# Products of probs and values issued in four runs per group of heads instead of ten single steps

## What is computed

```python
qkv = xn @ w_qkv.T + b_qkv                       # q, k, v: (2, 1024, 32, 16)
scores = einsum('bqhd,bkhd->bhqk', q, k) / 4 + alibi
scores = where(causal, scores, -1e9)
out = einsum('bhqk,bkhd->bqhd', softmax(scores), v)
s = out @ w_out.T + b_out
g = silu(octonion_ffn(xn, w_gate, w_up, w_down))
return x + s * g
```

## Time and profile before

| what | value |
|---|---|
| median of 3 runs | 965.25 us |
| the profiled execution, its own time | 966.12 us |
| its span, first to last instruction | 964.3 us |
| mean granted TensorE clock | 0.98 |
| TensorE busy | 905.3 us, 94% |
| VectorE busy | 648.4 us, 67% |
| ScalarE busy | 462.2 us, 48% |

### The profile page before, as it was taken

One profiled execution on the slowest core, in us unless ns is written; L12 is line 12 of the kernel. 1 busy time (PEld: TensorE's weight loads), 2 busy tenths in 40 slices (PEclk: granted clock), 3 DMA queues, 4 the chain that ended last, 5 costly groups with the idle time before them and its releaser, 6 DMA issues.

```text
span 964.3 us, 16724 instructions
## 1 busy us (share of the span) xinstructions
PE 905.3 (94%) x5630; PEld 483.2 (50%) x5630; DVE 648.4 (67%) x1425; ACT 462.2 (48%) x634; POOL 110.8 (11%) x119
## 2 busy tenths in 40 slices
PE   3696999999999996999999999999999999999987
PEld 3582457645854682444444444444444444443565
DVE  5678543543454442774888888888888888883488
ACT  3474532243223311124666666666666666667610
POOL 1121212130313032120000000000000000000042
PEclk9798999999999998999999999999999999999999
DMA  7322004201410138911256664546664456742757
GB/s 199 148 83 77 1 25 154 85 1 38 164 60 0 58 139 119 126 17 44 41 75 102 100 84 73 78 72 100 95 86 74 77 74 100 99 134 102 246 180 306
DMA packets 78177, 92.41 MB, mean 96 GB/s; under 512 B 26829, under 2 KB 43213, under 8 KB 78129
## 3 DMA queue, kind: packets, MB, share of 16 engines
q1 hardware_dynamic: 78017, 91.54, 43.7%
q0 software_dynamic: 112, 0.27, 0.2%
HBM read 57.57 MB, written 33.82 MB: 95 GB/s over the span
## 4 chain that ended last, share of the span: by engine, by line
PE 51%; DMA 3%; DVE 3%; issue 2%; ACT 1%; SPq 1%; DVEq 0%; ACTq 0%
PE psum L1285 15%; PE psum L1256 14%; PE psum L1269 12%; PE psum L1274 3%; DMA o_scr<-osum 2%; PE psum L250 2%; PE psum L251 2%; PE psum L1259 1%; PE psum L262 1%; PE psum L261 1%; DMA r_scr<-den 1%; DMA Ks<-r_scr 1%; ACT hid L278 1%; SPq L1022 0%; DVE mx L1150 0%
## 5 line engine op out<-in xcount | busy, mean ns | idle before, releaser
L1100 ACT ACTIVATE probs<-psum 128x1024 f32<-128x1024 f32 (+1 forms) x256 | 222.1, 915 | 108.3 <-PE psum L1274 91.1
L1150 DVE TENSOR_REDUCE mx<-psum 128x1 f32<-128x512 f32 (+2 forms) x352 | 224.8, 685 | 37.9 <-PE psum L1256 26.2
L1256 PE MATMUL psum<-Ks,Qs 99*128 99x512 bf16 (+3 forms) x768 | 203.8, 329 | 7.9 <-issue 5.6
L1269 PE MATMUL psum<-Qs,Ks 102*128 102x512 bf16 (+3 forms) x768 | 190.4, 326 | 2.1 <-DVE g_stage L306 1.6
L1146 DVE CUSTOM_DVE_ANT_0 mshown<-psum,ahead 128x384 bf16<-128x384 f32 (+1 forms) x256 | 149.2, 621 | 33.1 <-PE psum L1256 32.0
L250 PE MATMUL psum<-X,MG 128*128 128x512 f16 (+1 forms) x352 | 136.3, 387 | 5.0 <-PEq L324 3.7
L251 PE MATMUL psum<-X,MG 128*128 128x512 f16 (+1 forms) x352 | 136.1, 387 | 0.0
L1256 PEld LDWEIGHTS psum<-Ks,Qs 99*128 99x128 bf16 x768 | 62.5, 97 | 134.9 <-DVE mx L1146 51.5
L1285 PE MATMUL psum<-probs,Vs 128*32 128x512 f32 (+3 forms) x1152 | 126.2, 521 | 0.0
L1269 PEld LDWEIGHTS psum<-Qs,Ks 102*128 102x128 bf16 x768 | 73.8, 98 | 57.0 <-ACT probs L1100 8.4
L278 ACT ACTIVATE hid<-psum,sig_scale 128x512 f32<-128x512 f32 (+1 forms) x44 | 30.2, 687 | 146.7 <-PE psum L251 146.6
(11 more groups left out here) (128 smaller groups left out, 1128.5 us busy)
## 6 DMA issues: line engine op xcount, KB each, us to landing
Qs<-q_scr SPq DMA_DIRECT2D x96, 128.0 KB
Ks<-k_scr SPq DMA_DIRECT2D x96, 128.0 KB
o_scr<-osum SPq DMA_DIRECT2D x32, 256.0 KB, 4.1
q_scr<-qk_stage SPq DMA_DIRECT2D x16, 384.0 KB, 2.4
k_scr<-qk_stage SPq DMA_DIRECT2D x16, 384.0 KB, 2.5
v_scr<-v_stage SPq DMA_DIRECT2D x16, 256.0 KB, 2.0
g_scr<-g_stage SPq DMA_DIRECT2D x16, 256.0 KB, 2.0
Vs<-v_scr SPq DMA_DIRECT2D x16, 256.0 KB
```

The lines of the kernel that those rows point to most:

```text
L1100: nc.scalar.activation(probs[n % PSLOTS][:, 2 * pair:2 * pair + 2, 0:COLS[n]], s_bank[pair][:, :, 0:COLS[n]], ACT.Exp, scale=1.0 / INV_SCA ...
L1150: nc.vector.tensor_reduce(dst, m_bank[bank][:, 0:n * keys].rearrange("p (n k) -> p n k", n=n), AX.X, ALU.max).then_inc(max_read, 1)
L1256: last = nc.tensor.matmul(tile[:, hh, :], Qs[s][0:ROWS_MAX, h + hh, qb * P:(qb + 1) * P], Ks[s][0:ROWS_MAX, h + hh, k0:k0 + keys], start=( ...
L1269: last = nc.tensor.matmul(bank[:, at:at + cols], Ks[s][0:ROWS_ALL, 2 * pair + h, kb * P:(kb + 1) * P], Qs[s][0:ROWS_ALL, 2 * pair + h, (c ...
```

## The change

The products of a group are issued in four runs. A run is one item of the order, so that neither scores nor maximum tiles stand between its products. Run (8, 9) of the group before stands behind S1b, run (0, 1, 2) behind S4b, run (3, 4) behind S6b, and run (5, 6, 7) behind S9b. What each item computes, the buffers and all waits are the same. `copy_out` stands where it did (step 2 and step 5).

```diff
-LAG = 3
+RUNS = {1: (1, (8, 9)), 4: (0, (0, 1, 2)), 6: (0, (3, 4)), 9: (0, (5, 6, 7))}
...
-        if n >= LAG:
-            main.append(("products", 0, n - LAG, 4 * COLS[n - LAG]))
-        elif not first:
-            main.append(("products", -1, NST + n - LAG, 4 * COLS[NST + n - LAG]))
+        ago, run = RUNS.get(n, (0, ()))
+        if run and not (first and ago):
+            main.append(("products", -ago, run, sum(4 * COLS[m] for m in run)))
...
-                        if n == LAG - 1 and not first:
+                        if n == 2 and not first:
                             copy_out(t - 1, 1, ENDS[1])
-                        if n == ENDS[0] + LAG:
+                        if n == 5:
                             copy_out(t, 0, ENDS[0])
...
                         elif kind == "products":
-                            products(t + a, b, (s + a) % SLOTS)
+                            for n in b:
+                                products(t + a, n, (s + a) % SLOTS)
...
-                for n in range(NST - LAG, NST):
+                for n in RUNS[1][1]:
                     products(QUADS - 1, n, (QUADS - 1) % SLOTS)
```

## The result

| | us |
|---|---|
| before, median of 4 runs | 965.21 (963.32 to 968.9) |
| after, median of 4 runs | 1045.65 (1044.37 to 1050.88) |
| ratio after to before | 1.083 (1.0783 to 1.0877) |
| profiled execution after: its own time, span, mean clock | 1050.88, 1049.1, 0.973 |

The kernel became 8.3% slower; 1045 us had been forecast. The profiled execution is the longest of the four (the others 1044.37 to 1045.97), and its mean clock is the lowest (0.973 against 0.977 to 0.979). By these means it ran at half clock for 57 us in all and the others for 44 to 48 (an estimate: twice the share that is missing, times the span), at most 4 to 6 us of work: as much as it is longer.

The account below looks back on a forecast made before the run. TensorE was taken as full and the bound, so only its start-to-start times count. Per group 6.85 us of waits less 1.60 of drains gave +5.25, in all +80 us, 1045 us, range 1012 to 1062 (own bounds 1031 to 1053).

Parts of the forecast that it names:

- The drains: Product pieces on TensorE: each costs 0.27 us beyond its columns; ten become four, saving 1.60 us per group.
- The waits: TensorE waiting for ScalarE, VectorE and the maxima's transfer: 6.85 us per group, less 1.60 saved, +5.25.
- S1a and S1b: Score halves of step 1: TensorE waits for ScalarE 0.37 us each, 0.74 together.
- S3a, S3b, S4a, S4b: Score halves in the longest stretch, steps 2 to 4: waits for ScalarE of 0.25, 0.27, 0.78, 0.27, together 1.57 us.
- M27 and M28: Maximum tiles behind run (0, 1, 2): five tiles for three banks, waits for VectorE 0.53 and 0.39, together 0.92 us.
- M36 and M38: Maximum tiles behind run (3, 4): waits for VectorE's banks of 0.46 and 0.15, together 0.61 us.
- S8b: Score half in steps 7 to 9: TensorE waits 0.57 us for ScalarE.
- in front of the next group: Behind run (5, 6, 7): first score waits 1.87 us for the maxima's transfer, bank waits of M8 to M10 included.
- The whole: Groups 1 to 13 +68.2, group 0 +3.4, group 14 +5.5, group 15 and last products +2.8: +80 us, 1045 us.
- A: Rival: stalls stay hidden and only the drains go, 25 us less, 940 us; chance 0.05.
- B: Rival: only ScalarE's waits are real, VectorE's banks and the transfer never hold TensorE, +32, 997 us; chance 0.07.
- C: Rival: granted clock falls behind the wait in front of every group, 25 us more, 1070 us; chance 0.05.

Follow-up runs that it names:

- both short kernels: Exponentials and maximum reads cut to 64 columns: changed kernel with the maxima's transposition before the last run, 943.22 us; old order of ten single pieces, 962.05 us.
- the kernel with both readers short: Changed kernel with exponentials and maximum reads cut to 64 columns and the maxima's transposition ahead of run (5, 6, 7): 943.22 us, 27.62 per group.
- short reads and R ahead: Changed kernel with VectorE reading 64 columns per maximum tile row and the maxima's transposition ahead of run (5, 6, 7): 991.92 us, ratio 1.026.
- faster reads: Changed kernel with VectorE reading only 64 columns of each maximum tile row, order unchanged: 1032.39 us, ratio 1.0683.
- short exponentials: Changed kernel with ScalarE taking the exponential of only 64 columns of each head: 1000.62 us, ratio 1.0355.
- six runs with the old order in groups 14 and 15: Six runs instead of four, maximum tiles placed by hand, but groups 14 and 15 back to single pieces: 955.41 us, ratio 0.9875.
- R ahead: Changed kernel with the transposition of the finished maxima issued ahead of run (5, 6, 7) instead of behind it: 1030.22 us, ratio 1.0645.
- both kernels with six runs: Changed kernel with six runs and hand-placed maximum tiles, 959.69 us; the same with single pieces again in groups 14 and 15, 955.41 us.
- tiles spread: Changed kernel, same four runs, but the rule spreading maximum tiles counts the products' columns a quarter: 984.35 us, ratio 1.0177.
- four runs placed: Changed kernel, same four runs, but maximum tiles of groups 0 to 13 placed by a handwritten list: 972.36 us, ratio 1.0052.

## Why the prediction was right

**The drains, 1.60 us.** Right: a run pays one overhead of 0.17 us at its end (0.18 forecast) and 0.09 in front, whatever its length; both short kernels differ by 1.34 us, and small waits make up the rest. The Trainium skill ("TensorEngine Tiling (Array Packing)", Key Properties) has the array drain when the tiling mode changes; that agrees with a cost that goes by the number of changes and not by the work between them. That the cost is this drain is not shown: at the same places the type changes too, from bf16 to fp32 and back, and no run separates the two.

**The waits, 6.85 us.** Right one by one. Start to start in group 6: S1a and S1b 0.37 and 0.35 (0.37 each forecast), S3a, S3b, S4a, S4b 0.26, 0.25, 0.75, 0.26 (0.25, 0.27, 0.78, 0.27), M27 and M28 0.52 and 0.37 (0.53, 0.39), S6a and S6b 0.26 and 0.31 (0.25, 0.32), M36 and M38 0.45 and 0.09 (0.46, 0.15), S8b 0.50 (0.57), and in front of the next group 0.15 + 0.28 + 0.25 + 1.23 = 1.91 (1.87). The sum is 6.65. The group took 34.15 us, 34.2 forecast. Without these waits it would be 27.50, which is 0.15 more than the 27.35 that are the work of the kernel with both readers short; that rest is not accounted for. What made the forecast possible is that the old order leaves two of the handovers visible: ScalarE's in the last group, which waits for it, and the transfer's in the one weight load that it held. VectorE's was taken to be the same 0.06 us as ScalarE's, without a row for it, and the waits of M27 and M28 came out right with it.

**The whole.** Groups 1 to 13 brought +69.0 us in the profiled execution (68.2 forecast), of which 1.7 is the clock. Group 0 +4.2 (3.4), group 14 +6.6 (5.5) and group 15 with the last products +4.4 (2.8): these three were under-sized by 3.5 us together. At least part of it is the clock, 0.90 in the mean of group 14; how much is the order was not separated. The first stage moved by 0.8 us, the tail behind the last copy by 0.1. That the median is 1045.65 is therefore partly a coincidence: the span of the profiled execution grew by 84.8 us and not by 80, and the other three were 5 us shorter than it, most likely because the clock fell less often in them (by their mean clocks, see above); they were not profiled.

**The rivals.** A (only the drains go) is what the kernel with both readers short shows, and would have needed such readers. B (only ScalarE's waits are real) falls: transfer and banks cost 3.16 us of the 6.53. Its price was right: with both taken away, by short reads and R ahead, the kernel takes 991.92 us, 997 forecast. C (the clock) was given too little. The prediction took an idle time of 1.82 us with a clock of 1.00 behind it as a sign that waits of that length are safe. That was the weak step: one event. A wait of 0.9 to 1.1 us was followed by a fall in 2 of 14 cases and the one of 1.65 us in 12 of 14. It cost this kernel under 2 us in the loop, and with faster reads it took more than half of their gain there (groups 1 to 13 became 7.3 us shorter, 16.9 had been expected). The Trainium skill ("TensorE: Matmul & The Clock Gate", What's actually happening) has the gate follow how busy the engine has been of late; the falls behind these waits agree. Why equal waits amid the same work differ, no run here shows.

## What to carry to other kernels

In an in-order queue the place of small work decides more than the size of the pieces: other places for the 39 small items, most of them 0.2 us long, were worth 5.4 us per group, merging pieces at most 1.6. Before work is gathered into longer runs, ask for each reader how much it can hold (two score banks, three tile banks) and what lies between two of its inputs once the run is gone. A matmul of 0.06 us that starts a chain over a copy and a DMA should be issued more than 3 us before its result is needed (3.02 us passed here from its start), and a look at that path in the trace before (one wait of 0.16 us, so no slack) tells in advance who will be late next.

## What the runs showed of the hardware

- Short pauses can be followed by a fall of TensorE's clock: single idle times of 0.9 to 1.1 us, once per group of 34 us, were followed by 3.4 us at 0.50 in 2 of 14 cases (with short exponentials in 3 of 14), idle times of 1.5 to 1.7 us in 12 of 14. In front of R in group 14 an idle time of 2.07 us came with a fall of 3.4 or 6.8 us in all five kernels that have it, one of 1.82 us in neither of two (before, and six runs with the old order in groups 14 and 15).
- In five kernels every third group takes 0.1 to 0.4 us more (32.98 and 33.35 with R ahead; 30.99 and 31.3 with short reads too; 27.62 and 27.9 with both short; 28.06 and 28.2 in both kernels with six runs). Three groups are one turn of the loop. In the kernel before, with tiles spread and with four runs placed all groups are alike (28.96, 30.04, 28.77); in the changed one nothing of it shows in front of the wait for the transfer. In the kernel with both readers short it is a wait of 0.31 us (once 0.42) of TensorE in front of the first score behind the turn, for nothing that the profile shows; that it is the branch of the loop was not tested.
- Two ACTIVATEs in a row are 0.92 us apart where one shows 1.02, two tile reads 0.60 where one shows 0.69. The spacing and not the duration sets the rhythm, and the sums of the prediction go by it.
